# First-layer products and gelus of two mixture-of-experts stages issued several pairs ahead through a ring of buffers

## The reference, cut to what matters

```python
# first mixture stage, H = 128 (called m1 in the kernel)
logits = einsum('bsd,de->bse', xn, Wr) + br
top_vals, top_idx = top_k(logits, 2);  w = softmax(top_vals)
w_full = scatter of w to the 8 experts
for e in range(8):
    h = gelu(einsum('bsd,dh->bsh', xn, W1[e]) + b1[e])
    y = y + (einsum('bsh,hd->bsd', h, W2[e]) + b2[e]) * w_full[..., e, None]
# second mixture stage, H = 64 (called m2)
probs = softmax(tokens @ router_w.T);  rw, re = top_k(probs, 2);  rw = rw / sum(rw)
for e in range(8):
    out = out + combine[:, e] * (gelu(tokens @ w1[e] + b1[e]) @ w2[e] + b2[e])
```

## Time and profile before

| | |
|---|---|
| median of 3 runs | 705.5 us |
| lowest and highest | 704.82 and 707.24 us |
| profiled execution, whole time | 704.32 us |
| its span | 702.5 us |
| PE, DVE, ACT, POOL busy | 585.7, 487.0, 309.4, 251.5 us |
| first mixture stage (m1) | from about 232.7 to 345.5 us of the span |
| second mixture stage (m2) | from about 485.0 to 568.4 us of the span |

### The profile page before, as it was taken

How to read it: one execution, slowest core, us unless ns; L and a number is a source line. 1 busy time by engine, 2 the same in 40 slices (tenths; PEclk the granted TensorE clock), 3 DMA queues, 4 the chain that set the end, 5 groups by cost and what they waited for, 6 DMA issues and landing times. The chain is left out here.

```text
span 702.5 us, 13106 instructions
## 1 busy us (share of the span) xinstructions
PE 585.7 (83%) x4758; PEld 385.9 (55%) x4758; DVE 487.0 (69%) x1352; ACT 309.4 (44%) x659; POOL 251.5 (36%) x220
## 2 busy tenths in 40 slices
PE   3996676978878879898898999998786878988886
PEld 2674565855653432322386788886332233987553
DVE  0235677767667597778747888677758897955695
ACT  1331332656646545344325555522233437953164
POOL 6734992213001210101146677543311137900150
PEclk9998897999995599999999999998799999999998
DMA  6876621020000200000100000003200010000002
GB/s 188 239 225 181 191 84 71 10 66 1 1 1 0 80 1 0 1 1 0 41 2 15 9 15 9 14 2 72 78 1 0 1 41 0 3 3 2 0 1 61
DMA packets 18944, 30.06 MB, mean 43 GB/s; under 512 B 6466, under 2 KB 15810, under 8 KB 18242
## 3 DMA queue, kind: packets, MB, share of 16 engines
q1 hardware_dynamic: 16322, 19.81, 9.8%
q0 software_dynamic: 2560, 9.44, 4.5%
HBM read 27.26 MB, written 1.05 MB: 40 GB/s over the span
## 5 line engine op out<-in xcount | busy, mean ns | idle before, releaser
L177 POOL TENSOR_TENSOR norm_rstd<-norm_var,minus_half 128x16 f32<-128x16 f32 x16 | 47.0, 2940 | 186.5 <-DVE norm_var L171 186.5
L1395 ACT ACTIVATE m_g<-PS,w_slot 128x512 f32<-128x512 f32 x96 | 60.8, 685 | 87.9 <-PE PS L1446 87.8
L1340 DVE TENSOR_TENSOR m_gw<-m_g,PS 128x512 f32<-128x512 f32 x96 | 60.9, 675 | 15.1 <-ACT m_g L1395 7.5
L1446 PE MATMUL PS<-m_xT,w_slot 64*128 64x512 f32 x192 | 62.2, 656 | 0.6 <-ACT m_g L1395 0.5
L1470 PE MATMUL PS<-m_gw,w_slot 128*64 128x512 f32 x192 | 55.1, 643 | 1.2 <-DVE m_gw L1340 1.2
L106 PE MATMUL PS<-w_base 128*128 128x128 f32 x330 | 48.3, 294 | 1.4 <-DVE win_obias L1671 1.4
L106 PEld LDWEIGHTS PS<-w_base 128*128 128x128 f32 x330 | 40.2, 151 | 8.7 <-issue 6.0
L1454 PE MATMUL PS<-m_gT,m_sel 48*128 48x512 bf16 x96 | 25.1, 405 | 19.5 <-DVE m_gw L1340 15.6
L147 DVE BATCH_NORM_STATS2 norm_halves<-H 128x6 f32<-128x64 f32 x256 | 34.3, 210 | 3.4 <-PEq L2888 3.1
L1454 PEld LDWEIGHTS PS<-m_gT,m_sel 48*128 48x128 bf16 x96 | 5.9, 93 | 53.4 <-DVE m_gw L1340 42.0
L261 POOL DMA_INDIRECT tok_windows<-in_emb,tok_ids x32 | 30.5, 952 | 11.2 <-issue 9.4
(11 more groups left out here) (341 smaller groups left out, 1496.2 us busy)
## 6 DMA issues: line engine op xcount, KB each, us to landing
rff_routed<-in_routed SPq DMA_DIRECT2D x64, 129.0 KB, 2.5
w_slot<-in_w_rat SPq DMA_DIRECT2D x1, 1525.0 KB, 12.0
w_slot<-in_w_win SPq DMA_DIRECT2D x1, 1378.5 KB, 5.8
w_slot<-in_w_m SPq DMA_DIRECT2D x1, 1329.0 KB, 5.8
w_slot<-in_w_early SPq DMA_DIRECT2D x1, 1100.0 KB, 5.0
rat_inv<-in_rat_taps SPq DMA_DIRECT2D x1, 1024.0 KB, 7.5
rat_hf<-in_rat_taps SPq DMA_DIRECT2D x1, 1024.0 KB, 9.2
out<-H SPq DMA_DIRECT2D x8, 128.0 KB, 2.2
```

The lines of the kernel that those rows point to most:

```text
L177: nc.gpsimd.tensor_tensor(N.rstd[:], N.var[:], C.minus_half[:], ALU.pow).then_inc(S["norm_rstd"], 1)
L1340: nc.vector.tensor_tensor(gw[:, i % 2, half, :], g[:, i % 2, half, :], gate_bank[half], ALU.mult)\
L1395: nc.scalar.activation(g[:, i % 2, half, :], hid_bank[(n - 1) % 3], ACT.Gelu, bias=b1[:, s:s + 1])\
L1446: nc.tensor.matmul(hid_bank[n % 3], w1[lane(half), s, :], pair_of(xT, pair)[lane(half)], start=True, stop=True).then_inc(S["hid_ps"], 1)
```

## The change

`g` becomes a ring of `lead` slots, 6 in m1 and 4 in m2. The gelus and `hidden` of step i+lead are issued in the loop at step i, by ACT ahead of its copies and by PE in the place where `hidden(i+2)` stood. The first `lead` steps of both are issued in the opening. The buffers `gw`, `gate_bank`, `y_bank` and `hid_bank` keep their sizes, and `gates` stays one step ahead.

In the opening, `turn_parts(0)` comes after `lead-2` steps of `hidden`, and two more follow before `gates(0)`. Two of the three `rouse` calls go (10 or 24 transposes, and 8). The leftover transforms of m1 stand behind `hidden(0)` and `hidden(1)`, the moves behind `gelus(0)` and `gelus(1)`, and the two `add_squares` move from the opening into DVE's loop, behind `gw` of steps 0 and 1.

```diff
+LEAD = {128: 6, 64: 4}
@@
-        g = sb("g", [P, 2, 2, PAIR])
+        g = sb("g", [P, lead, 2, PAIR])
@@ DVE
-            if again:
-                for s in range(SQUARED_TAIL, STEPS):
-                    C.denominators.add_squares(v, s)
             for k in range(2):
                 expand(0, k)
@@
-                    nc.vector.tensor_tensor(gw[:, i % 2, half, :], g[:, i % 2, half, :], gate_bank[half], ALU.mult)\
+                    nc.vector.tensor_tensor(gw[:, i % 2, half, :], g[:, i % lead, half, :], gate_bank[half], ALU.mult)\
                         .then_inc(S["gw"], 1)
+                if again and i < STEPS - SQUARED_TAIL:
+                    C.denominators.add_squares(v, SQUARED_TAIL + i)
@@ ACT
-            if again:
-                for s in range(SQUARED_TAIL, STEPS):
-                    C.denominators.move(act, s, spare_banks[s % 2])
-            for i, (pair, s) in enumerate(steps):
+            def gelus(i):
                 for half in range(2):
                     n = 2 * i + half + 1
                     act.wait_ge(S["hid_ps"], n)
-                    if i >= 2:
-                        act.wait_ge(S["gw"], n - 4)
+                    if i >= lead:
+                        act.wait_ge(S["gw"], n - 2 * lead)
...
+            for i in range(lead):
+                gelus(i)
+                if again and i < STEPS - SQUARED_TAIL:
+                    C.denominators.move(act, SQUARED_TAIL + i, spare_banks[i % 2])
+            for i, (pair, s) in enumerate(steps):
+                if i + lead < len(steps):
+                    gelus(i + lead)
                 if s == 1 and pair >= 1:
                     copy_output(pair - 1)
@@ PE
             def hidden(i):
                 pair, s = steps[i]
+                if s == 0:
+                    pe.wait_ge(S["xT"], pair + 1)
@@
-            if again:
-                for s in range(SQUARED_TAIL, STEPS):
-                    C.denominators.transform(pe, C, s, spare_banks[s % 2])
-            hidden(0)
-            rouse(nc, C, opening_bank, 10 if again else 24)
-            hidden(1)
+            for i in range(lead - 2):
+                hidden(i)
+                if again and i < STEPS - SQUARED_TAIL:
+                    C.denominators.transform(pe, C, SQUARED_TAIL + i, spare_banks[i % 2])
             pe.wait_ge(S["identb"], 1)
             turn_parts(0)
+            for i in range(lead - 2, lead):
+                hidden(i)
             if again:
                 pe.wait_ge(C.denominators.moved, STEPS)
-            rouse(nc, C, gate_bank[1], 8)
@@
-                if i + 2 < len(steps):
-                    hidden(i + 2)
+                if i + lead < len(steps):
+                    hidden(i + lead)
```

More of the change, by code:

```diff
@@ L1183, in gelu_moe @@
     plan = AHEAD[hid]
+    lead = LEAD[hid]
     with ExitStack() as ctx:
@@ L1383, in _ @@
             nc.scalar.copy(sel[:], C[pre + "_sel"]).then_inc(S["sel"], 1)
-            for k in range(2):
-                copy_x(0, k)
-            if again:
-                for s in range(SQUARED_TAIL, STEPS):
-                    C.denominators.move(act, s, spare_banks[s % 2])
-            for i, (pair, s) in enumerate(steps):
+            def gelus(i):
                 for half in range(2):
@@ L1392, in _ @@
                     act.wait_ge(S["hid_ps"], n)
-                    if i >= 2:
-                        act.wait_ge(S["gw"], n - 4)
-                    nc.scalar.activation(g[:, i % 2, half, :], hid_bank[(n - 1) % 3], ACT.Gelu, bias=b1[:, s:s + 1])\
-                        .then_inc(S["gelu"], 1)
+                    if i >= lead:
+                        act.wait_ge(S["gw"], n - 2 * lead)
+                    nc.scalar.activation(g[:, i % lead, half, :], hid_bank[(n - 1) % 3], ACT.Gelu,
+                                         bias=b1[:, steps[i][1]:steps[i][1] + 1]).then_inc(S["gelu"], 1)
+            for k in range(2):
+                copy_x(0, k)
+            for i in range(lead):
[5 more added lines that the diff above has]
+                    gelus(i + lead)
                 if s == 1 and pair >= 1:
```

## The result

The changed kernel takes 712.4 us (median of 6 runs, 709.9 to 713.6), the kernel before 705.2 us beside it. The ratio is 1.0092, with a 95% interval from 1.0061 to 1.0123: slower by 0.9%, 6.5 us by the ratio. (The ratio isn't the quotient of the two medians, which is 1.010 here; both lie in the interval.) The forecast was 709.5 us with a range from 703.5 to 712.8. A second set of eight runs of the changed kernel, taken beside the last experiments, gave 1.0088 [1.0058, 1.0117].

A forecast was written before the change was run, and what follows sets the result against it. Neither DVE nor PE fills its loop; they take turns in waiting, and DVE bounds m1's start. m1 +3.1 and m2 +0.9 us on 704.3 gave 708.3, plus 1.2 for the median: 709.5 us, range 703.5 to 712.8.

The forecast's parts named there:

- worse than the forecast: Rival, chance 0.15: low clock through both openings and once more in each loop, 1.9 us each, giving 713.3 us.
- The sum: Whole kernel: m1 +3.1 us and m2 +0.9 us, together +4.0 us on the profiled execution's 704.3.
- Opening of m1: m1 before its loop: turn_parts waits behind hidden(3), which needs gelus(2) behind move 7; gw(0) ends 2.5 us later.
- the two cases: m1's opening: shift of +2.5 us, or +1.65 if the high clock comes earlier and ACT's own chain binds.
- Squares: m1's first steps: the two add_squares now stand behind gw(0) and gw(1), where DVE is busy, +1.2 us.
- Gelu waits: m1's loop: the two places where DVE's gw waited for a gelu go with the ring, -2.8 us.
- The wait at turn_output: m1 steps 9, 17, 25: PE waits 0.85 us for copy_output behind the new gelus, +2.6 us in all.
- End of m1: Last four steps of m1: each loses a hidden step but DVE's 2.00 us takes over, -0.4 us.
- m2: Second stage: +0.5 us left of the later opening, +0.85 at turn_output of step 9, -0.4 at the end: +0.9 us.
- the clock pays it back: Rival, chance 0.20: low clock stretches in the loops and openings go, -4.0 us against +4.0, giving 705.5 us.
- DVE runs through: Rival, chance 0.07: the short gelu buffer holds DVE back, m1's loop shrinks to DVE's own work, giving 694.5 us.
- they filled waits for DVE: m2's opening: the removed transposes cost nothing before, as they filled waits for DVE; no term in the sum.

The follow-up runs named there:

- e8: Changed kernel with both openings in the order of the kernel before, including its 10 or 24 rouse transposes: 1.0048 of the kernel before, 709.3 us.
- e2: Changed kernel with the two add_squares back in DVE's opening, ahead of expand: 1.0083 of the kernel before.
- e5: Kernel before with only ACT's copy_x of round 1 one step later in its queue, no ring: 0.9895 of the kernel before, 696.9 us.
- e1: Changed kernel with copy_output ahead of gelus(i+lead) in ACT's loop: 1.0054 of the kernel before, 710.7 us.
- e4: Changed kernel with m1 as in the kernel before, so only m2 is changed: 0.9987 of the kernel before.
- e7: Changed kernel with four steps of lead in m1 instead of six, m2 unchanged: 1.0060 of the kernel before, 708.3 us.
- e12: Changed kernel run once more without any edit, as reference: 1.0088 of the kernel before.
- e10: Changed kernel with openings and transposes of before, lead of four, add_squares in the opening and copy_output ahead of the gelus: 0.9946 of the kernel before, 700.2 us.
- e6: Kernel before without the two rouse calls (transposes) in the openings, nothing else changed: 1.0015 of the kernel before.
- e11: Kernel before with copy_x later, turn_parts(0) ahead of hidden(1), and m1's add_squares in steps 9 and 10: 0.9984 of the kernel before.

## Why the prediction was right, and where it was off

The direction, the stage and most terms were right. The range held the time by 0.4 us: 712.4 under a bound of 712.8, which was set that high for half of the rival *worse than the forecast*. The sum was +4.0 us on the profile and the profile shows +7.9 of span: m1 +6.9 where 3.1 stood, m2 +1.0 where 0.9 stood, and nothing elsewhere.

- **Opening of m1**: +2.5 us forecast. In the trace of the changed kernel +6.3, and 4.1 to 6.3 over four traces. This is the step that failed. The place was right (the second half of hidden(3) behind move 7 and gelus(2), `turn_parts` behind it, DVE idle), the size was not. The working took 1.9 to 2.0 us a step up to hidden(1) and the transforms, but let hidden(2) end at 248.8, and gave half-products of hidden(3) to hidden(5) 0.95 us each. That is the clock of before, which had risen at 248.1. The transposes that stood ahead of that rise were among the lines removed. With it low to 258.3, hidden(2) and hidden(3) took 4.9 us and hidden(4) and hidden(5) 4.7, where the working has 3.7 and 2.6. Also the two cases were set wrongly: 2.5 and 1.65 were both cases in which the clock rises, and neither was the bound for one in which it doesn't. e8 gives the rest: even at the high clock the four steps cost 3.4 us, 0.9 over the forecast, for half-products in turn take 1.4 us a step. The other 0.7 to 2.9 us are the low clock and the moves.
- **Squares**: +1.2 forecast, 1.2 measured (11.32 against 10.10 us over the first four `gw`, and undone in e2).
- **Gelu waits**: -2.8 forecast, -2.8 measured. The distance to the changed kernel's `gw` shrinks from 7.5 us at the fourth `gw` to 4.7 at step 10 (286.97 against 280.98, less 1.24). The waits of `gw` for a gelu in m1 are gone. e5 gets the same 2.7 us with no ring.
- **The wait at turn_output**: 0.85 forecast, 0.82 measured each time, three in m1. e1 shows that they were on the path: m1 from the first `gw` on is 2.7 us shorter, for three waits of 0.82. What the two in m2 cost, its trace doesn't show.
- **End of m1**: -0.4 forecast. From the third `turn_output` to the last `gw` it is 9.35 us (340.58 to 349.93) where it was 9.84 (331.92 to 341.76): -0.5.
- **m2**: +0.9 forecast, 0.9 in the trace of the changed kernel; 0.3 to 1.1 in the five traces of it as changed (with e4, e7, e2 and e12). Its opening came near to the +2.5 of the working: counted from `turn_parts`, the first `gw` is 2.0 us later than before in this trace and 2.4 to 3.0 in the other four. The working has 4.75 us for hidden(2) and hidden(3), and it was 3.8 here, as the clock rose at 510.9, ahead of the last half-products. A wait that wasn't in the sum, 0.91 us of `turn_x` for `copy_x` behind gelus(7), is of the kind of the `turn_output` wait. By the time of e4 none of it can be measured.
- **Rivals**: that the clock pays it back was the opposite of what came; in m1 the low stretches in the loop were two more than before, and in e12 one as before. *Worse than the forecast* named what came in m1, the low clock through the opening and again in the loop, but gave that opening nothing beyond the same 2.5 us; that its 713.3 lies near the 712.4 is luck. That DVE runs through is out: `gates` waited fourteen times for `gw` as before, so the rule on repeated gaps and too few buffers (the Trainium skill, Perfetto Trace Analysis, Optimization Strategy) didn't apply to this ring. e7 and e10 agree, where a ring of four is no worse than one of six. Whether more gate banks would take those fourteen waits away, no run here tests.

The forecast erred to the low side in good part because of removed lines that I had costed at nothing, "they filled waits for DVE". They filled waits, but they also brought the clock up. By the trace of e6 that was worth 1.8 us up to the logits of m1 in the kernel before, with 1.0015 [0.9991, 1.0039] for the time. It was worth more together with the other part of the change, which put more PE work ahead of `gates(0)`: in m2, from `turn_parts` to the first `gw`, 0.2 us in the kernel before (e6) and 1.2 to 2.1 us with the ring (e8). Cost and cover were judged one at a time.

## What to carry to other kernels

Look at what stands ahead of a stalled instruction in its queue before deepening the buffer that it waits for: here a copy that waited 2.5 us stood ahead of gelus whose products were ready, and putting it one step later gave 0.9 to 1.0%, where the ring with its filling lost 0.9%. Transposes that only keep the clock up look like waste in a busy table; before taking them out, look at what the clock does behind them. Filling a ring ahead of the loop isn't free when the engine that fills it is the one that must release the loop; put only as much ahead as fits beside the other engine's work, and before the instruction that this one waits for. If every producer call in a loop runs n steps ahead, all that stands behind it in the same queue becomes as late as its newest input.

## What the runs showed of the hardware

A hidden product is two halves, each on 64 of the array's 128 rows. Both together took 0.95 to 1.02 us at 2.4 GHz and 2.0 us at 1.2 GHz; one alone took 1.1 (271.31) and 2.0 us, as long as both.

In the changed kernel's opening PE shows no idle time from 240.5 to 258.3, with hidden products on 64 rows a half, transforms on 32 and four bf16 `turn_parts`, and the granted clock was 1.2 GHz all the while. In e8, with ten transposes over all 128 rows from 243.4 on, it was 2.4 GHz from 246.3. The Trainium skill (TensorE: Matmul & The Clock Gate, Part 1: The HAM clock gate) says that the slow clock is the default and that sustained matmul activity releases it. e8 agrees; the 17.8 us of the changed kernel do not fit it as it stands. In two other traces of the same opening (e1 and e2) the clock rose 5.7 us sooner in the stage, also with no such transposes, and in e11 it rose only 18.7 us from the start of the stage, with the ten transposes and a wait of 0.84 us behind them. What sets these apart, no run here separates.

The same opening in four traces of the same order brought the clock up at 18 to 24 us from the stage's start, and the first `gw` at 22.4 to 24.7 us. Times of the kernel before spread over some 10 us (700.6 to 710.7 in 29 runs), those of the changed kernel over 5 (708.6 to 713.6 in 14), and a term of a microsecond is told by the trace, not by the time. The traces spread too: the stages ahead of m1, which no run changes, took from 231.4 us (e8) to 236.2 us (e4).
